# A state-space scan beside experts on one core: exponentials batched by two pairs, rows of B and z moved, norms on GpSimd

## Chip, cores and metric

The kernel runs on one core of one Trainium2 chip. The metric is the device time of one execution in microseconds; the median of three runs is shown for the kernel before. A profile is one execution of its own.

## What is computed

The input x has 2048 tokens of 128 features. Two layers follow each other, each with an attention-like half and a feed-forward half, and ahead of each half a layer norm with a modulation; each half's result is gated and added to x. Cut to what matters here:

```
h = layernorm(x)*(1+ca)+sa ; x = x + ga * retention_and_ffn(h)        # layer 0, first half
h = layernorm(x)*(1+cb)+sb ; x = x + gb * experts(h)                  # layer 0, second half: 8 experts, top 2
h = layernorm(x)*(1+ca')+sa' ; x = x + ga' * mamba(h)                 # layer 1, first half
h = layernorm(x)*(1+cb')+sb' ; x = x + gb' * spectral_product(h)      # layer 1, second half

mamba(h):  xz = h @ W_in.T ; x_val, z = split(xz) ; x_val = silu(conv4(x_val))
           dt = softplus(h[:, :64] @ W_dt.T + b) ; B = h @ W_B.T ; C = h @ W_C.T     # 16 states
           state_n = exp(dt*A_n) * state_n + dt*x_val*B_n      # along the tokens, 256 channels, n = 0..15
           y = sum_n state_n * C_n ; return (y * silu(z)) @ W_out.T
experts(h): p = softmax(h @ w_router) ; out = sum over the top two of p_e * (gelu(h@w1_e + b1_e) @ w2_e + b2_e)
```

## The kernel before, in words

The tokens are cut into four chunks of 512. After layer 0's first half, which is done for all chunks, the rest is one long software pipeline written out by hand in program order on every engine: `later_stages()` (from L255) yields a pair number p, from -12 to 31, and for each p the list of extra stages that run in it. Each engine walks the same list and does its share in order; semaphores tie the engines together.

In pair p two things run side by side.

- **Experts.** Group g = p + 12 is one expert for one chunk (32 groups, so they run in pairs -12 to 19). TensorE makes the hidden layer in four parts k: `up(g, k)` (L1211 on) is three matmuls of 512 columns into one of two banks `pH`. ScalarE's `hidden` (L966) turns each part to gelu, `gel` (L973), a ring of six tiles. `down(g, k)` (L1223 on) multiplies it by the second weights into `pO`: two down products are 16 matmul records of 128 columns in the trace (the line is L1231). VectorE's `moe_acc(g - 1)` (L727, its line L732) adds the previous group's result into X; `down(g, 0)` waits for `moe_acc(g - 1)`. A third `up` waits for the first gelu of its group, since there are two banks.
- **Scan.** Chunk c = p // 8, k = p % 8 covers the states 2k and 2k+1, so pairs 0 to 31 hold four chunks of eight pairs. ScalarE's `decays(p)` (L976) makes the four tiles exp(dt*A), dA (L985; two states by two halves of the channels). TensorE's `row_b(m)` (L1291, matmul L1299) copies row m of B to all partitions of one bank `pB`; VectorE's `products(m)` (L743, L748) multiplies it with u = dt*x into `pCT`; `scans(m)` (L751, L761) does two scans into Hs. GpSimd's `output(p, o)` (L363, L382) multiplies by a row of C (Crow, brought by SyncE's DMAs) to Z. In pairs below ALONE = 20 GpSimd then issues an accumulating DMA, `add_up` (L387, L396), that adds Z to Acc; from pair 20 on TensorE's `total` (L1301 on) adds Z up in PSUM.

The order on VectorE in a pair is product, two scans, `moe_acc(g-1)`, product, two scans, with extra stages between. On TensorE it is given by `pair` (from L1235): two up products, `row_b(2p+1)`, two up products, then `row_b(2p+2)` if the pair has a TensorE stage at place A ("early"), the stages at A, two down products, `row_b(2p+2)` if it wasn't early, the stages at B, two down products, the stages at C. On ScalarE it is four gelus, `decays(p+1)`, then stages at A and B, the norm's application, stages at C. Exp, gelu, silu and softplus are in different tables, so each change between them comes with an ACT_TABLE_LOAD.

The extra stages, for chunk c's tail (chunk c-1 after its scan) and front (chunk c+1 before its scan), by k: tail: `gate` (1), `project` (2, A), `tail_x`, `ln_stats` (2), norm applied and turned (3), `fft` (4, B). Front: norm statistics (4), applied and turned (4, C), the convolution `x_part` (5 A and 6 A), `rows` for B and C (5 B), `dt_part` (6 B, C), `step` (7, makes u), `z_part` (7 A, B). A layer norm goes: VectorE statistics (L538, L541), GpSimd 1/sqrt in four small instructions (`ln`, L347 to L354), ScalarE applies it (`ln_apply`, L830, line L835), TensorE turns it (L1029), ScalarE evacuates it into h4T. For `rows`, ScalarE copies B and C to BCf (L950) and casts them to ST (L952), and GpSimd splits them by four instructions (L479 to L482) before `row_b` can use them.

After pair 31 a serial tail follows for the last chunk: total, gate (L772), projection (L1334), norm, spectral products (L1342), store.

## Time and profile before

| | |
|---|---|
| median of 3 runs | 605.51 us (605.38 to 606.65) |
| profiled execution | 606.43 us |
| its span, first to last instruction | 604.4 us |
| mean granted TensorE clock | 0.948 |
| busy: PE, DVE, ACT, POOL | 482.4, 428.9, 363.4, 313.2 us |
| scan stretch, first product to last scan | 263.5 to 583.0 us of the span |

PE is TensorE, DVE VectorE, ACT ScalarE, POOL GpSimd, SP SyncE. Busy time is the time in which an engine runs an instruction; matmuls are pipelined and their ends are modelled, so of a run of matmuls the starts say more. The granted clock is TensorE's share of full speed: 1.00 is 2.4 GHz, 0.50 is 1.2 GHz. "idle before, releaser" is how long the engine stood before an instruction, and what ended that. The busy shares are averages over stretches with different limits, so the rows below are taken from single stretches.

### The profile page before, as it was taken

The numbers are of one execution on the slowest core, as the hardware profiler recorded it, in microseconds if no ns is written. First come the engines' busy times: TensorE is split into PE (matmuls) and PEld (weight loads), VectorE is DVE, ScalarE is ACT, GpSimd is POOL, SyncE is SP. The second block draws the span as 40 slices with busy tenths as digits, with TensorE's granted clock in tenths as the row PEclk, the third lists the DMA queues.
The fourth block names the chain that finished last, engine by engine and source line by source line (L and its number), as shares of the span: only waits on it lengthen the run. The fifth ranks groups of instructions, "written<-read, shape, count | busy, mean of one in ns | idle before, by whom it ended". The sixth has DMA issues, their size and how long they took to land.

```text
span 604.4 us, 6869 instructions
## 1 busy us (share of the span) xinstructions
PE 482.4 (80%) x2346; PEld 337.7 (56%) x2346; DVE 428.9 (71%) x723; ACT 363.4 (60%) x507; POOL 313.2 (52%) x220
## 2 busy tenths in 40 slices
PE   3869876769899999979869988789897497667573
PEld 3457544434588886757756677657586443233222
DVE  4766798964534334058997779997879985997961
ACT  0531442224664676689999999799988656634201
POOL 3224976866111011314686649767557946566541
PEclk9986999989999999999999989999989779897797
DMA  8700000000000000401866553765725703111000
GB/s 294 272 1 0 1 1 1 2 0 0 1 0 2 2 1 0 142 1 35 193 147 139 151 139 87 180 136 144 168 75 148 165 20 104 70 63 42 17 0 17
DMA packets 15010, 44.74 MB, mean 74 GB/s; under 512 B 2241, under 2 KB 7745, under 8 KB 12545
## 3 DMA queue, kind: packets, MB, share of 16 engines
q0 software_dynamic: 2448, 17.83, 14.5%
q1 hardware_dynamic: 11952, 25.57, 12.4%
q10 hardware_dynamic: 576, 0.92, 0.5%
q8 instruction: 18, 0.29, 0.2%
q14 instruction: 16, 0.12, 0.1%
HBM read 25.31 MB, written 1.18 MB: 44 GB/s over the span
## 4 chain that ended last, share of the span: by engine, by line
PE 24%; ACT 13%; DVE 12%; issue 6%; POOL 3%; DMA 3%; POOLq 0%; ACTq 0%; DVEq 0%
DVE Hs L761 6%; PE pO L1231 5%; DVE pCT L748 4%; ACT dA L985 3%; PE pY L1274 3%; PE pY L1317 3%; ACT gel L973 3%; PE pH L1219 2%; ACT L985 2%; ACT L973 2%; PE pH L1221 2%; PE pH L1220 2%; ACT ln_x L835 2%; PE pH L1274 2%; DMA Acc<-ZS 1%
## 5 line engine op out<-in xcount | busy, mean ns | idle before, releaser
L1231 PEld LDWEIGHTS pO<-w_e,gel 128*128 128x128 f32 x1024 | 124.8, 195 | 14.2 <-issue 8.8
L1231 PE MATMUL pO<-w_e,gel 128*128 128x128 f32 x1024 | 127.2, 279 | 1.4 <-DVE X L732 1.1
L761 DVE TENSOR_TENSOR_SCAN Hs<-dA,HL,pCT 128x512 f32<-128x512 f32 x96 | 117.7, 1268 | 8.1 <-POOL Zev L382 3.8
L382 POOL TENSOR_TENSOR ZS<-Hs,Crow 128x1024 f32<-128x1024 f32 x32 | 76.5, 2392 | 58.3 <-DVE Hs L761 58.3
L973 ACT ACTIVATE gel<-pH,b_e 128x512 f32<-128x512 f32 x128 | 85.9, 687 | 33.3 <-PE pH L1221 32.6
L985 ACT ACTIVATE dA<-dt,a_neg 128x512 f32<-128x512 f32 x128 | 81.9, 710 | 21.0 <-DVE Hs L761 20.7
L748 DVE TENSOR_TENSOR pCT<-u,pB 128x1024 f32<-128x1024 f32 x64 | 78.3, 1224 | 16.7 <-PE pB L1299 15.5
L1219 PE MATMUL pH<-h2h,w_e1h 128*128 128x512 f32 x128 | 57.8, 452 | 22.6 <-ACT gel L973 21.4
L382 POOL TENSOR_TENSOR Zev<-Hs,Crow 128x1024 f32<-128x1024 f32 x26 | 62.8, 2420 | 16.0 <-DVE Hs L761 15.2
L732 DVE SCALAR_TENSOR_TENSOR X<-pO,wts,X 128x128 f32<-128x128 f32 x128 | 35.9, 343 | 43.2 <-PE pO L1231 43.1
L438 POOL TENSOR_TENSOR ZA<-Qsb,S 128x1024 f32<-128x1024 f32 x16 | 38.0, 2374 | 33.6 <-DVE S L656 32.0
L1221 PE MATMUL pH<-h2h,w_e1l 128*128 128x512 f32 x128 | 51.0, 398 | 0.0
L1220 PE MATMUL pH<-h2l,w_e1h 128*128 128x512 f32 x128 | 50.7, 396 | 0.0
L1299 PE MATMUL pB<-ST,sel 96*128 96x512 bf16 x64 | 25.7, 401 | 30.4 <-DVE pCT L748 27.3
L1219 PEld LDWEIGHTS pH<-h2h,w_e1h 128*128 128x128 f32 x128 | 24.1, 188 | 38.6 <-ACT gel L973 34.4
L835 ACT ACTIVATE ln_x<-X,ln_nb,ln_rs 128x128 f32<-128x128 f32 x48 | 19.7, 480 | 36.8 <-POOL ln_nb L354 36.8
L761 DVE TENSOR_TENSOR_SCAN Hs<-dA,pCT 128x512 f32<-128x512 f32 x32 | 37.3, 1207 | 3.8 <-ACT dA L985 2.1
L899 ACT COPY Qsb<-pCT 128x1024 f32<-128x1024 f32 x16 | 16.2, 1013 | 37.2 <-PE pCT L1107 37.2
L1106 PE MATMUL pH<-qk_hi,pick 128*128 128x512 f32 x32 | 16.7, 523 | 23.5 <-DVE S L656 23.5
L973 ACT ACT_TABLE_LOAD x26 | 33.4, 1283 | 0.5
L1299 PEld LDWEIGHTS pB<-ST,sel 96*128 96x128 bf16 x64 | 6.3, 99 | 47.6 <-DVE pCT L748 37.0
L656 DVE TENSOR_TENSOR_SCAN S<-cols,S,pH 128x512 f32<-128x512 f32 x24 | 30.7, 1280 | 0.8
(225 smaller groups left out, 878.1 us busy)
## 6 DMA issues: line engine op xcount, KB each, us to landing
Crow<-c_rows SPq DMA_DIRECT2D x32, 512.0 KB, 4.0
Acc<-ZS POOLq DMA_DIRECT2D x10, 1024.0 KB, 8.5
Acc<-Zev POOLq DMA_DIRECT2D x7, 1024.0 KB, 7.7
w_e<-in_w_e SPq DMA_DIRECT2D x2, 2048.0 KB, 10.4
X<-in_x SPq DMA_DIRECT2D x4, 256.0 KB, 7.0
out<-h2T SPq DMA_DIRECT2D x4, 256.0 KB, 2.2
S<-in_w_mod ACTq DMA_DIRECT2D x2, 384.0 KB, 4.7
w_cx<-in_conv_row SPq DMA_DIRECT2D x1, 512.0 KB, 9.7
```

The source lines that it names most:

```text
L382: pool.tensor_tensor(Z, Hs[:, 2 * o:2 * o + 2, 0:w], Crow[:, 2 * (p % NCB) + o:2 * (p % NCB) + o + 1, 0:w].to_broadcast([P, ND, w]), ALU.m ...
L438: pool.tensor_tensor(ZA[:, :, :], Qsb[:, 2 * (R % 2):2 * (R % 2) + 2, :], S[:, 2 * r:2 * r + 2, :], ALU.mult).then_inc(s["att_zo"], 1)
L732: ins = vec.scalar_tensor_tensor(Xj, pO[:, j * P:(j + 1) * P], wts[:, c, j * E + e:j * E + e + 1], Xj, ALU.mult, ALU.add)
L748: vec.tensor_tensor(pU[:, :, 0:w], half_of(u, c), pB[:, None, 0:w].to_broadcast([P, ND, w]), ALU.mult).then_inc(s["mam_ub"], 1)
L761: vec.tensor_tensor_scan(Hs[:, 2 * o + d, 0:w], dA[:, 4 * (p % 2) + 2 * o + d, 0:w], pU[:, d, 0:w], HL[:, d, n:n + 1] if c else 0.0, ALU.m ...
L973: nc.scalar.activation(gel[:, n % NG, 0:w], pH[n % 2][:, 0:w], ACT.Gelu_apprx_tanh, bias=b_e1[:, NK * e + k:NK * e + k + 1]).then_inc(s["m ...
L985: nc.scalar.activation(dA[:, 4 * (p % 2) + r, 0:WIDTHS[c]], half_of(dt, c)[:, r % 2, :], ACT.Exp, scale=a_neg[:, r % 2, n:n + 1]).then_inc ...
L1219: mm(pH[n % 2][:, 0:w], w_e1h[:, g % E, part], h2h[:, c, 0:w], start=True, stop=False)
L1220: mm(pH[n % 2][:, 0:w], w_e1h[:, g % E, part], h2l[:, c, 0:w], start=False, stop=False)
L1221: mm(pH[n % 2][:, 0:w], w_e1l[:, g % E, part], h2h[:, c, 0:w], start=False, stop=True).then_inc(s["moe_h"], 1)
L1231: ins = mm(pO[:, j * P:(j + 1) * P], gel[:, n % NG, j * P:(j + 1) * P], w_e2[:, NK * (g % E) + k, :], start=(k == 0 and j == 0), stop=(k = ...
L1299: mm(pB[:, 0:w], sel[:, n:n + 1].to_broadcast([96, P]), ST[:, c % 2, 0:w], start=True, stop=True).then_inc(s["mam_bB"], 1)
```

## The change

- `decays`: in odd pairs p ScalarE does the exponentials of pairs p+1 and p+2, in even pairs none. dA has three slots in place of two, taken by p % 3, and decays(p) waits for the scans of pair p-3, not p-2.
- TensorE's `row_b(2p+2)` comes ahead of all down products also in every even pair.
- `z_part` leaves pair 7 of the chunk before and comes in pair 1 of its own chunk (A and B).
- GpSimd applies the norms (four subtract-and-multiply instructions of 128 columns); two of its small instructions go. It also casts BCf to ST.
- The front's norm is turned in pair 5 at a new place "U", behind `row_b(2p+1)` and between the second and third up product; on ScalarE its evacuation stands between the second and third gelu.
- Zev, ZS and Acc (two slabs) become one tile Zt with three slabs: slab 1 for odd pairs; the accumulator of chunk c and the Z of its even pairs use slabs 0 and 2 in turn. So the first output of a chunk waits for the accumulating DMA of the pair two back, and the output of pair k = 2 waits until the previous chunk is gated.

```diff
-        dA = sb("dA", [P, 2 * 2 * ND, TC])
+        dA = sb("dA", [P, 3 * 2 * ND, TC])
         Hs = sb("Hs", [P, 2 * ND, TC])
-        Zev = sb("Zev", [P, 2 * ND, TC])
-        ZS = sb("ZS", [P, 2 * ND, TC])
+        Zt = sb("Zt", [P, 3, 2 * ND, TC])
...
-            return (2 if p < ALONE else 0) + int(at == "B")
+            return (2 if p < ALONE else 0) + int(at in ("B", "U"))
...
+        def acc_of(c):
+
+            return Zt[:, 2 * (c % 2), :, 0:WIDTHS[c]]
+
+        def z_of(p):
+
+            c, k = divmod(p, NP)
+            if k == 0 and not alone(p):
+                return acc_of(c)
+            return Zt[:, 1 if k % 2 else 2 - 2 * (min(c, ALONE // NP) % 2), :, 0:WIDTHS[c]]
...
@@ -263,16 +270,17 @@
                 plan = []
                 if 0 <= tail:
                     plan += [(1, "mid", "gate", tail), (2, "A", "project", tail), (2, "end", "tail_x", tail),
-                             (2, "end", "ln_stats", tail), (3, "apply", "ln_apply", tail), (3, "C", "ln_turn", tail, 2),
+                             (2, "end", "ln_stats", tail), (3, "C", "ln_turn", tail, 2),
                              (3, "end", "bias", tail), (4, "B", "fft", tail)]
                 if 0 <= front < NL:
-                    plan += [(4, "mid", "ln_stats", front), (4, "apply", "ln_apply", front), (4, "C", "ln_turn", front, 1),
+                    plan += [(4, "mid", "ln_stats", front), (5, "U", "ln_turn", front, 1),
                              (5, "A", "x_part", front, 0), (5, "B", "rows", front), (6, "A", "x_part", front, 1),
-                             (6, "B", "dt_part", front, 0), (6, "C", "dt_part", front, 1), (7, "mid", "step", front),
-                             (7, "A", "z_part", front, 0), (7, "B", "z_part", front, 1)]
+                             (6, "B", "dt_part", front, 0), (6, "C", "dt_part", front, 1), (7, "mid", "step", front)]
+                if c >= 0:
+                    plan += [(1, "A", "z_part", c, 0), (1, "B", "z_part", c, 1)]
                 for q in range(1, NL):
                     at = k - (p + AHEAD - 3 * (q - 1))
-                    plan += [(at, "mid", "ln_stats", q), (at, "apply", "ln_apply", q), (at + 1, "A", "ln_turn", q, 0),
+                    plan += [(at, "mid", "ln_stats", q), (at + 1, "A", "ln_turn", q, 0),
                              (at + 1, "B", "route", q), (at + 2, "A", "turn", q), (at + 2, "B", "weigh", q)]
...
             def ln(c):
                 J = blocks(c)
                 pool.wait_ge(s["ln_stats"], L[0] + 1)
-                pool.wait_ge(s["ln_xn"], L[0])
-                pool.tensor_scalar(ln_nm[:, 0:J], ln_mv[:, 0:J, 0], -1.0, None, ALU.mult)
                 link(pool.tensor_scalar(ln_ve[:, 0:J], ln_mv[:, 0:J, 1], EPS, None, ALU.add))
                 link(pool.tensor_tensor(ln_rs[:, 0:J], ln_ve[:, 0:J], mhalf[:, 0:J], ALU.pow))
-                pool.tensor_tensor(ln_nb[:, 0:J], ln_nm[:, 0:J], ln_rs[:, 0:J], ALU.mult).then_inc(s["ln_rstd"], 1)
+                pool.wait_ge(s["ln_tr"], L[0])
+                for j in range(J):
+                    ins = pool.tensor_scalar(ln_x[:, j, :], rows_of(X, c)[:, j, :], ln_mv[:, j, 0:1], ln_rs[:, j:j + 1],
+                                             ALU.subtract, ALU.mult)
+                ins.then_inc(s["ln_xn"], 1)
                 L[0] += 1
...
+                Z = z_of(p)[:, part, :]
                 if p >= ALONE + 2:
-                    Z = [Zev, ZS][p % 2][:, part, 0:w]
                     pool.wait_ge(s["mam_y"], totals(p - 2))
-                elif k == 0 and not alone(p):
-                    Z = Acc[:, c % 2, part, 0:w]
-                    if c >= 2:
-                        pool.wait_ge(s["mam_y2"], 2 * (c - 1))
-                else:
-                    Z = [Zev, ZS][p % 2][:, part, 0:w]
-                    if p >= 2 and o == 0 and sums(p - 2):
-                        pool.wait_ge(mam_s[p % 2], 16 * sums(p - 2))
+                elif p >= 2 and o == 0 and sums(p - 2):
+                    pool.wait_ge(mam_s[p % 2], 16 * sums(p - 2))
+                if k == 2 and c and p < ALONE + 2 and o == 0:
+                    pool.wait_ge(s["mam_y2"], 2 * c)
...
-                pool.wait_ge(s["mam_st0"], c + 1)
-                pool.wait_ge(s["ln_rstd"], L[0])
+                pool.wait_ge(s["mam_bcs"], c + 1)
+                pool.wait_ge(s["ln_xn"], L[0])
                 for name, count in done.items():
                     if count:
                         pool.wait_ge(s[name], count)
+                link(pool.tensor_copy(st, bc))
                 link(pool.tensor_tensor(st[32:64, :], bc[32:64, :], st[32:64, :], ALU.subtract))
                 link(pool.tensor_tensor(P1[64:96, 0:w], bc[64:96, :], st[64:96, :], ALU.subtract))
                 link(pool.tensor_tensor(bc[64:96, :], bc[64:96, :], st[64:96, :], ALU.subtract))
...
-                if p >= 2:
-                    act.wait_ge(s["mam_sc"], 4 * (p - 1))
+                if p >= 3:
+                    act.wait_ge(s["mam_sc"], 4 * (p - 2))
                 for r in range(4):
                     n = 2 * k + r // 2
-                    nc.scalar.activation(dA[:, 4 * (p % 2) + r, 0:WIDTHS[c]], half_of(dt, c)[:, r % 2, :], ACT.Exp,
+                    nc.scalar.activation(dA[:, 4 * (p % 3) + r, 0:WIDTHS[c]], half_of(dt, c)[:, r % 2, :], ACT.Exp,
...
             for p, stages in later_stages():
                 if 0 <= p + AHEAD < NL * E:
-                    hidden(p + AHEAD, range(NK))
-                if 0 <= p + 1 < NL * NP:
-                    decays(p + 1)
+                    hidden(p + AHEAD, (0, 1))
+                run(p, stages, "U")
+                if 0 <= p + AHEAD < NL * E:
+                    hidden(p + AHEAD, (2, 3))
+                for q in (p + 1, p + 2) if p % 2 else ():
+                    if 0 <= q < NL * NP:
+                        decays(q)
                 run(p, stages, "AB")
-                run(p, stages, ("apply",))
                 run(p, stages, "C")
...
@@ -1239,12 +1233,16 @@
                 if moe:
                     up(g, 0)
                     up(g, 1)
+                if any(at == "U" for at, *_ in stages) and not moe:
+                    run(p, stages, "U")
                 if 0 <= p < NL * NP:
                     row_b(2 * p + 1)
                 if moe:
+                    run(p, stages, "U")
+                if moe:
                     up(g, 2)
                     up(g, 3)
-                early = not moe or any(at == "A" and stage in mine for at, stage, *_ in stages)
+                early = not moe or p % 2 == 0 or any(at == "A" and stage in mine for at, stage, *_ in stages)
                 if moe and early and 0 <= 2 * p + 2 < NL * NS:
                     row_b(2 * p + 2)
```

The other lines rename Zev, ZS and Acc to `z_of(p)` and `acc_of(c)`, take out `ln_apply`, the cast on ScalarE, ln_nm, ln_nb and two semaphores, and put ln_xn in the place of ln_rstd in waits. The dA slot p % 3 stands in the scans (L761) too.

## Rows read from the trace of the kernel before

**Rows 1.** Scan stretch: us, busy us of PE, PEld, DVE, ACT, POOL; clock, DMA.

```profile
263.50:583.00 319.50, 256.35 (x1252) 176.26 (x1251) 277.24 (x383) 238.60 (x324) 201.68 (x125) 0.94 0.42 105
```

**Rows 2.** Timeline of VectorE: start us, us, instruction; first products and waits of single pairs.

```profile
275.92 1.23 DVE L748 TENSOR_TENSOR pCT<-u,pB 128x1024 f32<-128x1024 f32 x1 [1.69 <-PE pB L1299]
...
284.63 1.22 DVE L748 TENSOR_TENSOR pCT<-u,pB 128x1024 f32<-128x1024 f32 x1
...
293.17 1.22 DVE L748 TENSOR_TENSOR pCT<-u,pB 128x1024 f32<-128x1024 f32 x1
...
357.73 1.23 DVE L748 TENSOR_TENSOR pCT<-u,pB 128x1024 f32<-128x1024 f32 x1 [3.19 <-PE pB L1299]
...
504.99 2.45 DVE L761 TENSOR_TENSOR_SCAN Hs<-dA,HL,pCT 128x512 f32<-128x512 f32 x2 [3.45 <-POOL Zev L382]
```

**Rows 3.** Timeline of ScalarE in pair 2, to the load before pair 3.

```profile
288.10 1.27 ACT L973 ACTIVATE gel<-pH,b_e 128x512 f32<-128x512 f32 x2
289.84 1.37 ACT L973 ACTIVATE gel<-pH,b_e 128x512 f32<-128x512 f32 x2 [0.47 <-PE pH L1221]
291.23 1.28 ACT L985 ACT_TABLE_LOAD   x1
...
295.11 1.28 ACT L973 ACT_TABLE_LOAD   x1
```

**Rows 4.** Timeline of TensorE in the same pair: third up product, next group's first.

```profile
288.84 0.50 PE L1219 MATMUL pH<-h2h,w_e1h 128*128 128x512 f32 x1 [1.22 <-ACT gel L973]
...
294.03 0.48 PE L1219 MATMUL pH<-h2h,w_e1h 128*128 128x512 f32 x1
```

**Rows 5.** Timeline of ScalarE in pairs 5 and 6, and pair 7's first gelu.

```profile
323.15 1.28 ACT L940 ACT_TABLE_LOAD   x1
...
326.27 1.28 ACT L973 ACT_TABLE_LOAD   x1
327.56 1.27 ACT L973 ACTIVATE gel<-pH,b_e 128x512 f32<-128x512 f32 x2
...
340.95 0.69 ACT L973 ACTIVATE gel<-pH,b_e 128x512 f32<-128x512 f32 x1
```

**Rows 6.** Timeline of ScalarE in pair 7: z's silu and what follows.

```profile
347.97 1.28 ACT L964 ACT_TABLE_LOAD   x1
...
350.37 1.28 ACT L973 ACT_TABLE_LOAD   x1
```

**Rows 7.** Chain that ended last, in order of time: two down products; the projection.

```profile
336.27 1.78 PE pO L1231 x16
...
373.17 1.79 PE pY L1334 x16
```

**Rows 8.** Timeline of VectorE: expert accumulates of pairs 1 and 19.

```profile
279.78 1.11 DVE L732 SCALAR_TENSOR_TENSOR X<-pO,wts,X 128x128 f32<-128x128 f32 x4
...
467.08 1.12 DVE L732 SCALAR_TENSOR_TENSOR X<-pO,wts,X 128x128 f32<-128x128 f32 x4
```

**Rows 9.** Four stretches about two pauses of TensorE (columns as in 1).

```profile
310.00:313.00 3.00, 1.19 (x11) 1.00 (x9) 2.93 (x5) 3.00 (x7) 1.80 (x2) 1.00 0.54 109
313.00:316.00 3.00, 2.26 (x11) 1.53 (x11) 2.97 (x7) 2.17 (x3) 2.50 (x3) 1.00 0.22 44
350.50:353.50 3.00, 1.11 (x6) 0.93 (x6) 2.84 (x3) 2.52 (x4) 1.29 (x1) 1.00 1.02 216
354.00:357.00 3.00, 3.00 (x16) 3.00 (x15) 0.50 (x2) 2.87 (x5) 2.36 (x1) 0.50 0.27 55
```

**Rows 10.** Timeline of TensorE in pair 8: its first two down products.

```profile
353.95 3.53 PE L1231 MATMUL pO<-w_e,gel 128*128 128x128 f32 x16
```

**Rows 11.** Groups of GpSimd's instructions by line: busy us, mean ns.

```profile
L354 POOL TENSOR_TENSOR ln_nb<-ln_nm,ln_rs 128x4 f32<-128x4 f32 x12 | 2.4, 202 | 0.9
...
L450 POOL TENSOR_TENSOR w_out<-w_out,gates 128x256 f32<-128x256 f32 x1 | 0.7, 729 | 0.0
```

**Rows 12.** Timeline of the tail: the last norm applied by ScalarE.

```profile
595.11 1.65 ACT L835 ACTIVATE ln_x<-X,ln_nb,ln_rs 128x128 f32<-128x128 f32 x4 [24.62 <-POOL ln_nb L354]
```

More of the change, by code:

```diff
@@ L283, in later_stages @@
             for stage in (("A", "total", NL * NP - 1), ("end", "gate", last), ("A", "project", last), ("end", "tail_x", last),
-                          ("end", "bias", last), ("mid", "ln_stats", last), ("apply", "ln_apply", last),
+                          ("end", "bias", last), ("mid", "ln_stats", last),
                           ("A", "ln_turn", last, 2), ("A", "fft", last)):
@@ L395, in add_up @@
                     pool.wait_ge(mam_s[(p - 1) % 2], 16 * sums(p - 1))
-                pool.dma_start(Acc[:, c % 2, :, 0:w], [Zev, ZS][p % 2][:, :, 0:w], accum_op=ALU.add).then_inc(mam_s[p % 2], 16)
+                pool.dma_start(acc_of(c), z_of(p), accum_op=ALU.add).then_inc(mam_s[p % 2], 16)
             link(pool.memset(mhalf[:, :], -0.5))
@@ L497, in gate @@
                 for d in range(ND):
[L498 removed]
+                    pool.tensor_tensor(y2[:, d, 0:w], acc_of(c)[:, d, :], half_of(gz, c)[:, d, :],
                                        ALU.mult).then_inc(s["mam_y2"], 1)
@@ L534, in ln_stats @@
                 Xc = rows_of(X, c)
-                vec.wait_ge(s["ln_rstd"], L[0])
+                vec.wait_ge(s["ln_xn"], L[0])
                 L[0] += 1
@@ L828, in _ @@
             nc.scalar.activation(silu_c[:, :], cols[:, COL["c0"]:COL["c0"] + 2], ACT.Silu).then_inc(s["silu_c_ready"], 1)
-            def ln_apply(c):
-                act.wait_ge(s["ln_rstd"], A[0] + 1)
-                act.wait_ge(s["ln_tr"], A[0])
-                for j in range(blocks(c)):
-                    ins = nc.scalar.activation(ln_x[:, j, :], rows_of(X, c)[:, j, :], ACT.Identity,
-                                               bias=ln_nb[:, j:j + 1], scale=ln_rs[:, j:j + 1])
-                ins.then_inc(s["ln_xn"], 1)
-                A[0] += 1
             def ln(dest, c, m, b, high=None):
@@ L950, in rows @@
                 nc.scalar.copy(BCf[:, c % 2, 0:w], PS[b][0:96, 0:w]).then_inc(s["mam_bcs"], 1)
-                act.wait_ge(s["mam_bcs"], c + 1)
-                nc.scalar.copy(ST[:, c % 2, 0:w], BCf[:, c % 2, 0:w]).then_inc(s["mam_st0"], 1)
             def dt_part(c, d, b):
@@ L996, in run @@
                         continue
-                    if stage == "ln_apply":
-                        ln_apply(c)
-                    elif stage in ("ln_turn", "route", "turn", "x_part", "rows", "dt_part", "z_part"):
+                    if stage in ("ln_turn", "route", "turn", "x_part", "rows", "dt_part", "z_part"):
                         {"ln_turn": turned, "route": route, "turn": turn, "x_part": x_part, "rows": rows, "dt_part": dt_part,
@@ L1312, in total @@
                 first = k == 0 or p == ALONE
-                Z = [Zev, ZS][p % 2]
+                Z = z_of(p)
                 for o in range(2):
@@ L1316, in total @@
                     for d in range(ND):
-                        ins = mm(pY[d][:, 0:w], ident[:, :], Z[:, 2 * o + d, 0:w], start=(first and o == 0),
+                        ins = mm(pY[d][:, 0:w], ident[:, :], Z[:, 2 * o + d, :], start=(first and o == 0),
                                  stop=(k == NP - 1 and o == 1))
@@ L1323, in total @@
                         for o in range(2):
-                            ins = mm(pY[d][:, 0:w], ident[:, :], Acc[:, c % 2, 2 * o + d, 0:w], start=False, stop=False)
+                            ins = mm(pY[d][:, 0:w], ident[:, :], acc_of(c)[:, 2 * o + d, :], start=False, stop=False)
                 ins.then_inc(s["mam_y"], 1)
```

12 lines of the change are left out of this document (3 added, 9 removed).

## The prediction

> **What bounds the kernel now.** I read the busy table of the joint and lone scan stretches first [rows 1]: from the first product of pair 0 to the last scan of pair 31, 319.5 us pass, VectorE works in 277.2 of them and is the busiest engine by 20 us. So what a change can take out of this stretch is VectorE's idle time, 42.3 us; behind it lies a serial tail of 604.4 - 583.0 = 21.4 us. Next VectorE's own order in time [rows 2]: from pair 2's first product to pair 3's, 293.17 - 284.63 = 8.54 us pass, a plain pair without a pause. The pauses stand at the seams of the chunks: 1.69 us for a row of B ahead of pair 1, 3.19 us for one ahead of pair 9.
>
> That bound has little air under it. ScalarE in pair 2 [rows 3] goes from the first gelu (288.10) to the next pair's (296.40, behind the load at 295.11) in 8.30 us, with no pause but those for TensorE's up products: gelus until 291.23 (3.13), a table load and four exponentials until 295.11 (3.88), a load back until 296.40 (1.29). While ScalarE does the 5.17 us of exponentials and loads, TensorE does the down products, which it has begun some 2.2 us after the first gelu, and from 294.03 on the next group's first up products [rows 4]. So today one engine's work covers the other's in every pair.
>
> **Part 1, exponentials of two pairs in odd pairs.** Removed: one exp and one gelu load per two pairs, 2 x 1.28 = 2.57 us of ScalarE [rows 3]. The same eight exponentials remain. What matters is the chain. In an odd pair ScalarE needs 3.13 for gelus, then 1.29 + 2 x 2.59 + 1.29 = 7.76 for load, eight exponentials and load: 10.89 until the even pair's first gelu. In the even pair no exponential covers TensorE. The down products of a group come behind its last up products, which wait for its gelus; the next group's first up product comes behind the down products; so all is in series: first gelu to first up product of the next group 294.03 - 288.10 = 5.93 (row of B and down products in it), and 1.00 from an up product's start to its gelu (288.84 in [rows 4] to 289.84 in [rows 3]). That is 6.93. The new chain is 10.89 + 6.93 = 17.8 us for two pairs. Today's is 2 x 8.30 = 16.6, VectorE needs 2 x 8.54 = 17.1. Two loads go, and the chain gets longer, because TensorE's 5.9 us that lay beside the exponentials now lie behind them every second time. In plain pairs the bound passes from VectorE to this loop of ScalarE and TensorE.
>
> The loop from pair 1 to pair 19 is nine periods: 9 x 17.8 = 160.2. What stages add inside it: pairs 5 and 6, the conv's silu with load and the copy of B and C, 326.27 - 323.15 less the cast, 2.5; the evacuation of the turned norm between gelus, taken at 0.6; and pair 6, whose convolution and step products stand between its gelus and the next, 340.95 - 327.56 = 13.39 in place of 6.93 [rows 5], so 9.6, twice (pairs 13 and 14): 19.1. Pairs 9 and 10, the moved z's silu with its load, 350.37 - 347.97 = 2.4 [rows 6], and the projection ahead of pair 10's down products, 1.79 [rows 7]: 4.2, twice (17 and 18): 8.4. Pairs 11 and 12: evacuation 0.8, spectral products 0.9 (half as many matmuls as the projection): 1.7. Sum 189.4 us.
>
> Today VectorE's expert accumulate of pair 1 starts at 279.78 and that of pair 19 at 467.08, 187.3 apart [rows 8]. That is the point at which VectorE waits for the loop, so the change makes this stretch 189.4 - 187.3 = 2.1 longer, from a start that is 1.7 earlier (part 2). Net 0.4 later at pair 19.
>
> **The clock.** In that loop TensorE stands still between the even pair's first two up products and its first gelu: 10.89 less 2.2 (up products of the odd pair) plus 0.7, less some 5.7 of work, 3.7 us. In the trace a pause of 2.2 us, TensorE's wait to turn the norm behind pair 4, left the granted clock at 1.00 (2.4 GHz); the wait for pair 8's first gelu, some 2 us too, was followed by half of it (0.50, the 1.2 GHz level) [rows 9]. And the half group of down products behind that wait took 3.53 us [rows 10] in place of 1.78 [rows 7]. The trace prices one such fall at 1.75 at most, and at nothing if it lies inside the wait. A 3.7 us pause is longer than the one that cost this, and what follows it (up, down, up) is all in the loop. It comes in pairs 0, 2, 4, 8, 10, 12, 16 and 18. The 187.3 of today hold two such falls (pairs 8 and 16); the 189.4 hold none. Bounds 0 and 8 x 1.75 = 14; I take 1.0 each, since part of the low stretch can lie in the pause and VectorE has a little air in pairs 4 and 12: 8.0. TensorE: Matmul & The Clock Gate, section HAM oscillation — how this bites in real kernels, of the Trainium skill says that a kernel whose matmul groups are parted by waits pays the fall anew at every group, the extra being half of the throttled time. By that rule alone all eight would be paid in full, nearer the upper bound; the rows show one such pause that goes unpunished, and decide for less.
>
> **Part 2, row of B ahead of the down products in even pairs.** It takes away the waits that follow even pairs, 1.69 ahead of pair 1 [rows 2] and 3.19 ahead of pair 9. The first counts in full (1.7). The second is already inside the loop's sum. In plain pairs the row is in time either way. Cost: none on TensorE, which has the same matmuls in another order; if the product ahead is late the down products wait for it, under 1.3 us and hidden while VectorE waits for the loop.
>
> **Part 3, z in its own chunk's pair 1.** A move of 2.4 us of ScalarE and four matmuls from pair 7 to pair 9. It frees pair 8 and loads pair 9, both in the sum. In chunk 0 it leaves pair -1, where it makes room for the four extra exponentials (2.6 against 2.4). In chunk 3 it lies in a pair that VectorE bounds: nothing.
>
> **Part 4, norms and cast on GpSimd.** Per norm GpSimd loses two small instructions (0.5) and gets four of 128 columns. No row shows one. Bounds 0.20 (4 columns) and 0.73 (256 columns, two inputs) [rows 11]; I take 0.46, between them by columns: 1.8. Inside the loop GpSimd has room. In the tail it replaces 1.65 on ScalarE [rows 12] plus 0.6 of small ones and hand-overs: gain 0.4, bounds -0.8 and +1.2. GPSIMD Engine Reference, section Engine selection, of the Trainium skill says that with one input it is roughly as fast as VectorE, slow only with two; by that the tail would gain near 1 us. The cast costs GpSimd up to 1.15, ScalarE loses 0.62; in pair 21 the two about cancel. The third Z slab and the waits on the accumulating transfers add no wait that the loop does not cover. From pair 20 to the tail I take no change: there are no expert products and ScalarE has room.
>
> **Sum:** 0.4 + 8.0 - 0.4 = +8.0. The profiled execution took 606.43 (span 604.4), so 614.4; the median of the runs shown is 0.9 lower, 605.51, so **613.5 us**.
>
> **Rivals.** A: the clock holds, since TensorE's work shifts until no pause is long enough. For: the first two stretches of [rows 9], where a pause costs nothing. Against: its last two, and that the new pauses are longer. Then 0.4 - 0.4 and up to 2 us of slack that I rounded into the loop: 603 to 606, 604.
> B: the loop is not closed, because VectorE's order keeps TensorE fed and the saved loads and early rows are all that counts. Then the pauses at the seams go: 1.7, and at pairs 6 to 8 and 14 to 16 the 3.19 ahead of the next pair and some 1.4 for a late accumulate, 4.6 each: -11, 594.5. Against: the series of gelu, down product, up product in an even pair has no other way round.
> C: GpSimd's late rows of B and C. The copy that feeds them now stands behind eight exponentials (2.6 later), then five instructions, and two outputs behind them; VectorE's scan already waited 3.45 us for this in pair 23 [rows 2]. It decides once the outputs of pair 6 end later than that pair's down products, some 3 us from now; then +2 a chunk on top, 619.
> D: gains at the seams and losses in plain pairs cancel within 0.2%.
>
> **How the numbers follow.** Forecast 0.50, C 0.13: slower 0.63. A 0.19 and B 0.12 with a few hundredths for a shorter loop: faster 0.30 (A ends on the other side). D: 0.07. What this kernel's runs can tell from no change is about 0.2%, 1.2 us. Range: clock bounds put 605.5 to 619.4 around the sum; the low end takes in A and the near part of B, the high end most of C: 599 to 619. Slower holds most of the chance; its own range is 607 to 619.
>
> **What would show it.** The odd pair's first gelu to the next odd pair's: 17.8 to 19.5 us in plain pairs. ScalarE's waits for up products and VectorE's expert accumulate waiting for down products in odd pairs grow, waits for rows of B fall; stretches of half clock appear in pairs 2 and 4, where now there are none; table loads fall by some 20. Wrong, if the accumulate of pair 19 comes earlier than 465, or if VectorE runs the plain pairs at 8.54 still.

## The result and the profile after

Four runs of the changed kernel have a median of **631.25 us** (629.32 to 633.41), four of the kernel before beside them 606.08 us. The ratio is 1.0419 (95% interval 1.0387 to 1.0452): slower by 4.2%, where 613.5 us was forecast and the range ended at 619. The direction was right, the size about a third of what came, and 631 lies outside the range.

The profiled execution took 629.32 us with a span of 627.3, so 22.9 us more span than before. The page's busy rows, time slices and chain, of the kernel after:

```profile
span 627.3 us, 6814 instructions
...
PE 498.2 (79%) x2346; PEld 348.6 (56%) x2346; DVE 429.9 (69%) x723; ACT 314.9 (50%) x435; POOL 347.6 (55%) x248
...
PEclk9979998899899999987989997889988879887796
...
PE 46%; DVE 22%; ACT 17%; issue 6%; POOL 6%; DMA 1%; ACTq 0%; POOLq 0%; DVEq 0%
```

ScalarE works 48.5 us less (363.4 before) and VectorE 1.0 us more, so nothing got more work but GpSimd. The same 2346 matmuls keep TensorE busy 15.8 us longer (482.4 before). The chain that ended last, as the profile follows it back, has TensorE in 77 of the 185.5 us of the loop before and in 107 of the 207.1 us of the loop after (the loop is bounded below). Both point at TensorE as the place where the time went; the timelines show how.

The stretch of [rows 1], from the first product of pair 0 to the last scan (columns as there), and then the loop from pair 1's first gelu to pair 19's:

```profile
263.66:604.30 340.64, 269.92 (x1235) 184.49 (x1235) 278.48 (x383) 198.58 (x275) 219.32 (x140) 0.88 0.40 99
...
278.44:485.51 207.07, 173.33 (x937) 134.16 (x936) 162.30 (x249) 142.71 (x195) 135.15 (x90) 0.90 0.54 128
```

VectorE has the same work as in [rows 1] (278.48 and 277.24 us) in 340.64 in place of 319.50 us: its idle time went from 42 to 62 us. The loop took 207.07 us; between the same gelus of the kernel before (279.79 to 465.32) it is 185.53 us at a mean clock of 0.98, here 0.90. The accumulates that answer to [rows 8], in VectorE's timeline after:

```profile
277.75 1.13 DVE L739 SCALAR_TENSOR_TENSOR X<-pO,wts,X 128x128 f32<-128x128 f32 x4 [0.28 <-PE pO L1225]
...
486.96 1.12 DVE L739 SCALAR_TENSOR_TENSOR X<-pO,wts,X 128x128 f32<-128x128 f32 x4
```

So pair 1 comes 2.0 us earlier, pair 19 comes 19.9 later, and the end 22.9 later. The loss is in the joint pairs. Here is how one period of it looks, in ScalarE's timeline from pair 2 to pair 4 (it answers to [rows 3]):

```profile
291.61 1.26 ACT L966 ACTIVATE gel<-pH,b_e 128x512 f32<-128x512 f32 x2
294.03 0.69 ACT L966 ACTIVATE gel<-pH,b_e 128x512 f32<-128x512 f32 x1 [1.16 <-PE pH L1215]
295.31 0.69 ACT L966 ACTIVATE gel<-pH,b_e 128x512 f32<-128x512 f32 x1 [0.59 <-PE pH L1215]
301.39 1.37 ACT L966 ACTIVATE gel<-pH,b_e 128x512 f32<-128x512 f32 x2 [5.39 <-PE pH L1215]
303.12 1.38 ACT L966 ACTIVATE gel<-pH,b_e 128x512 f32<-128x512 f32 x2 [0.36 <-PE pH L1215]
304.52 1.28 ACT L978 ACT_TABLE_LOAD   x1
305.82 5.02 ACT L978 ACTIVATE dA<-dt,a_neg 128x512 f32<-128x512 f32 x8
310.85 1.28 ACT L966 ACT_TABLE_LOAD   x1
312.14 1.26 ACT L966 ACTIVATE gel<-pH,b_e 128x512 f32<-128x512 f32 x2
```

The reader sees both halves of the forecast's loop. From pair 3's first gelu to pair 4's 10.75 us pass with one short wait of 0.36 (forecast 10.89). From pair 2's to pair 3's 9.78 us pass (forecast 6.93, plus 1.0 for the clock), and ScalarE stands still for 5.39 of them, waiting for the next group's first up product. TensorE's timeline at the start of that even pair:

```profile
292.35 0.79 PE L1213 MATMUL pH<-h2h,w_e1h 128*128 128x512 f32 x1 [4.32 <-ACT gel L966]
292.94 0.63 PE L1214 MATMUL pH<-h2l,w_e1h 128*128 128x512 f32 x1
...
295.52 5.13 PE L1225 MATMUL pO<-w_e,gel 128*128 128x128 f32 x32
300.41 0.48 PE L1213 MATMUL pH<-h2h,w_e1h 128*128 128x512 f32 x1
```

TensorE waits 4.32 us for the gelu behind eight exponentials (forecast 3.7; in pairs 4 and 8 it is 3.70), and comes out of the pause at half clock. The ranges of the two legs (columns as in [rows 1]):

```profile
291.60:301.40 9.80, 9.05 (x43) 7.90 (x44) 5.07 (x9) 2.65 (x5) 5.11 (x3) 0.65 0.79 179
301.40:312.10 10.70, 7.78 (x50) 6.23 (x48) 9.94 (x22) 10.29 (x14) 6.04 (x4) 1.00 0.35 82
```

The even pair runs at a granted clock of 0.65, the odd one at 1.00. [Rows 9] had 1.00 as well as 0.50 behind two pauses of about 2 us; the second experiment below shows a loss in each of the eight pairs with a longer one (3.4 to 4.3 us).

### The profile page after: what moved, and what is told of

The parts are those of the page before. It is cut to its first block, busy times and chain, and to the rows that moved or that the text cites. A ratio compares the mean times of both kernels' runs of the same rounds, so it can differ in the third digit from the quotient of the medians.

```text
span 627.3 us, 6814 instructions
## 1 busy us (share of the span) xinstructions
PE 498.2 (79%) x2346; PEld 348.6 (56%) x2346; DVE 429.9 (69%) x723; ACT 314.9 (50%) x435; POOL 347.6 (55%) x248
## 4 chain that ended last, share of the span: by engine, by line
PE 46%; DVE 22%; ACT 17%; issue 6%; POOL 6%; DMA 1%; ACTq 0%; POOLq 0%; DVEq 0%
PE pO L1225 12%; ACT dA L978 6%; PE pY L1315 5%; PE pH L1213 4%; DVE S L663 4%; PE pH L1215 3%; DVE Hs L768 3%; PE pH L1214 3%; PE pY L1272 3%; ACT gel L966 3%; DVE pCT L755 3%; DVE pH L662 2%; POOL Zt L388 2%; ACT L966 2%; ACT L978 2%
## 5 line engine op out<-in xcount | busy, mean ns | idle before, releaser
L388 POOL TENSOR_TENSOR Zt<-Hs,Crow 128x1024 f32<-128x1024 f32 x64 | 153.0, 2392 | 106.7 <-DVE Hs L768 102.9
L1225 PEld LDWEIGHTS pO<-w_e,gel 128*128 128x128 f32 x1024 | 126.9, 199 | 12.7 <-issue 8.7
L755 DVE TENSOR_TENSOR pCT<-u,pB 128x1024 f32<-128x1024 f32 x64 | 78.4, 1224 | 23.1 <-PE pB L1297 22.4
L1213 PE MATMUL pH<-h2h,w_e1h 128*128 128x512 f32 x128 | 61.9, 484 | 37.8 <-ACT gel L966 36.8
L1215 PE MATMUL pH<-h2h,w_e1l 128*128 128x512 f32 x128 | 54.9, 429 | 0.0
L1214 PE MATMUL pH<-h2l,w_e1h 128*128 128x512 f32 x128 | 54.7, 427 | 0.0
L1315 PE MATMUL pY<-Zt,ident 128*128 128x512 f32 x96 | 52.3, 694 | 2.9 <-POOL Zt L388 2.9
L1297 PE MATMUL pB<-ST,sel 96*128 96x512 bf16 x64 | 27.9, 435 | 31.1 <-DVE pCT L755 27.4
L362 POOL TENSOR_SCALAR ln_x<-X,ln_mv,ln_rs 128x128 f32<-128x128 f32 x48 | 37.6, 793 | 1.3
L1315 PEld LDWEIGHTS pY<-Zt,ident 128*128 128x128 f32 x96 | 21.6, 227 | 27.9 <-issue 22.3
L1100 PE MATMUL pH<-qk_hi,pick 128*128 128x512 f32 x32 | 16.6, 519 | 22.0 <-DVE S L663 22.0
L845 ACT ACTIVATE h3T<-pH,mods 128x512 f32<-128x512 f32 x3 | 2.3, 777 | 59.6 <-PE pH L1023 59.6
## 6 DMA issues: line engine op xcount, KB each, us to landing
w_e<-in_w_e SPq DMA_DIRECT2D x2, 2048.0 KB, 10.5
```

Source lines behind the costliest of these rows:

```text
L362: ins = pool.tensor_scalar(ln_x[:, j, :], rows_of(X, c)[:, j, :], ln_mv[:, j, 0:1], ln_rs[:, j:j + 1], ALU.subtract, ALU.mult)
L388: pool.tensor_tensor(Z, Hs[:, 2 * o:2 * o + 2, 0:w], Crow[:, 2 * (p % NCB) + o:2 * (p % NCB) + o + 1, 0:w].to_broadcast([P, ND, w]), ALU.m ...
L755: vec.tensor_tensor(pU[:, :, 0:w], half_of(u, c), pB[:, None, 0:w].to_broadcast([P, ND, w]), ALU.mult).then_inc(s["mam_ub"], 1)
L1213: mm(pH[n % 2][:, 0:w], w_e1h[:, g % E, part], h2h[:, c, 0:w], start=True, stop=False)
L1214: mm(pH[n % 2][:, 0:w], w_e1h[:, g % E, part], h2l[:, c, 0:w], start=False, stop=False)
L1215: mm(pH[n % 2][:, 0:w], w_e1l[:, g % E, part], h2h[:, c, 0:w], start=False, stop=True).then_inc(s["moe_h"], 1)
```

## The experiments

**The batch of exponentials, undone and judged by itself.** One edit to the changed kernel, on ScalarE; all other parts stay:

```
-                for q in (p + 1, p + 2) if p % 2 else ():
+                for q in (p + 1,):
```

> The changed kernel with the exponentials of one pair in every pair again (the third dA slab, the early row of B, the moved z and GpSimd's norms and cast stay). Theory 1 (the closed ScalarE-TensorE loop of Part 1 with its clock falls is the whole loss): each odd pair to the next odd pair goes back from 20.3-20.7 us to about 17.1, first gelu of pair 1 to that of pair 19 from 207 to about 185, time 603 to 608 us. Theory 2 (GpSimd's norms and late rows, or z in pair 1, cost most): it stays above 620 us.

Measured: 603.2 us, ratio to the kernel before 0.9941 (0.9915 to 0.9968). One line is worth 28 us, and what is left of the change beats the kernel before. From pair 1's first gelu to pair 19's it is 181.94 us (277.89 to 459.83), at a mean granted clock of 1.00; theory 1 holds, and the stretch is 3 us shorter than its 185. Its plain pair 8, in ScalarE's timeline:

```profile
348.37 1.27 ACT L966 ACTIVATE gel<-pH,b_e 128x512 f32<-128x512 f32 x2
...
351.50 1.28 ACT L978 ACT_TABLE_LOAD   x1
352.80 2.56 ACT L978 ACTIVATE dA<-dt,a_neg 128x512 f32<-128x512 f32 x4
355.38 1.28 ACT L966 ACT_TABLE_LOAD   x1
356.67 1.27 ACT L966 ACTIVATE gel<-pH,b_e 128x512 f32<-128x512 f32 x2
```

A pair takes 8.30 us again, loads included. The two loads that the batch saves per two pairs (2.57 us) bought a period of 10.75 + 9.78 us in place of 16.6.

**The pauses filled.** Is the loss the longer loop or the clock? In even pairs, except those that hold the convolution, TensorE repeats its second up product five times before the real one (0.70 us each in the trace, 3.5 in all). The repeats write the same values to the same bank, which nobody reads before the last, so they only keep TensorE at work in the pause:

```
+                for _ in range(again):
+                    mm(pH[n % 2][:, 0:w], w_e1h[:, g % E, part], h2h[:, c, 0:w], start=True, stop=False)
+                    mm(pH[n % 2][:, 0:w], w_e1h[:, g % E, part], h2l[:, c, 0:w], start=False, stop=False)
+                    mm(pH[n % 2][:, 0:w], w_e1l[:, g % E, part], h2h[:, c, 0:w], start=False, stop=True)
...
-                    up(g, 1)
+                    up(g, 1, 5 if p % 2 == 0 and p % NP != 6 and p >= 0 else 0)
```

> The changed kernel, with TensorE repeating the second up product five times (5 x 0.64 = 3.2 us) in the pause of pairs 0, 2, 4, 8, 10, 12, 16, 18, ...; nothing else moves. Theory 1a (beyond the 17.8 us loop the loss is the clock, 1.6 to 3 us a fall): the half-clock stretches of these pairs go, plain periods fall from 20.3-20.7 to about 18.0 us, time 612 to 618 us. Theory 1b (the clock is a side effect, the loop is longer in itself): period stays at 20 us or more, time 629 us or more.

Measured: 616.48 us, ratio 1.0153 (1.0098 to 1.0209). More work on TensorE made the kernel 15 us faster. Its loop, and TensorE's timeline in pair 8:

```profile
277.58:472.42 194.84, 183.28 (x1042) 142.08 (x1041) 162.95 (x253) 143.37 (x194) 135.24 (x89) 0.99 0.57 132
```

```profile
355.10 0.50 PE L1217 MATMUL pH<-h2h,w_e1h 128*128 128x512 f32 x1 [0.21 <-ACT gel L966]
...
356.84 3.73 PE L1229 MATMUL pO<-w_e,gel 128*128 128x128 f32 x32
360.33 0.48 PE L1217 MATMUL pH<-h2h,w_e1h 128*128 128x512 f32 x1
```

The loop takes 194.84 us at a clock of 0.99 in place of 207.07 at 0.90. From the third up product to the next group's first one it is 360.33 - 355.10 = 5.23 us; in pair 2 of the changed kernel, above, 300.41 - 292.35 = 8.06. The legs (from a pair's first gelu to the next pair's) that start in an even pair, us:

| pair | 0 | 2 | 4 | 8 | 10 | 12 | 16 | 18 | sum |
|---|---|---|---|---|---|---|---|---|---|
| changed kernel | 8.54 | 9.78 | 9.75 | 8.28 | 11.23 | 9.30 | 9.55 | 10.28 | 76.7 |
| filled | 6.91 | 7.61 | 7.50 | 6.94 | 9.26 | 8.33 | 6.94 | 9.26 | 62.8 |

The difference is 14.0 us in eight legs, 1.75 each. The plain even legs of 6.91 and 6.94, with the odd legs of 10.76 to 10.78, are the forecast's full-clock loop: 17.7 where 17.8 was forecast.

The repeats don't reach a ninth fall. In pair 13 TensorE waits for VectorE ahead of a row of B, in the changed kernel and in the filled one, and the convolution's products behind it run at half clock. The batched kernel with the norms on ScalarE and the row late (its run stands further down) has the same wait and stays at 1.00. TensorE's timelines of the changed kernel, the filled one, and that one:

```profile
417.58 0.39 PE L1297 MATMUL pB<-ST,sel 96*128 96x512 bf16 x1 [1.83 <-DVE pCT L755]
417.81 5.30 PE L1272 MATMUL pY<-h3T,w_cx 128*128 128x512 f32 x8
```

```profile
408.09 0.39 PE L1301 MATMUL pB<-ST,sel 96*128 96x512 bf16 x1 [1.83 <-DVE pCT L755]
408.31 5.29 PE L1276 MATMUL pY<-h3T,w_cx 128*128 128x512 f32 x8
```

```profile
416.67 0.39 PE L1312 MATMUL pB<-ST,sel 96*128 96x512 bf16 x1 [1.84 <-DVE pCT L755]
416.90 3.60 PE L1287 MATMUL pY<-h3T,w_cx 128*128 128x512 f32 x8
```

The leg of pair 13 is 15.25 us in the first two and 13.56 in the third: 1.7 us for this fall.

**Only half of them filled.** The same with `p in (0, 2, 4, 8)` as the condition.

> The changed kernel with the five repeats of the second up product only in pairs 0, 2, 4 and 8; the pauses of pairs 10, 12, 16 and 18 stay empty. Theory 1 (each fall has its own price, paid in its own pair): pairs 0, 2, 4, 8 take 6.9 to 7.6 us from first gelu to the next pair's, pairs 10, 12, 16, 18 stay at 9.3 to 11.2; about half of the filled kernel's gain, 622 to 626 us. Theory 2 (the repeats help in another way, by moving the whole loop against GpSimd and VectorE once): over 80% or under 20% of that gain.

Measured: 620.74 us, ratio 1.0237 (1.0188 to 1.0285). The filled pairs take 6.94, 7.58, 7.49 and 6.93 us, the empty ones 11.62, 9.42, 9.67 and 10.30: each fall is paid in its own pair, by 7.4 us in these four legs against 14.0 in all eight. The total of 620.74 us lies below theory 1's range, and its gain, 10.5 of 14.8 us or 71%, fits neither theory; in the profiled executions 1.8 us of it arose ahead of pair 0, which is no effect of the edit (its first gelu starts at 268.13, in the changed kernel at 269.90). So the legs answer the question, for theory 1, and the total alone would not.

**The norms back on ScalarE**, each at its old place, the cast still on GpSimd. The central lines of the edit:

```
-                for j in range(J):
-                    ins = pool.tensor_scalar(ln_x[:, j, :], rows_of(X, c)[:, j, :], ln_mv[:, j, 0:1], ln_rs[:, j:j + 1],
-                                             ALU.subtract, ALU.mult)
+                for j in range(blocks(c)):
+                    ins = nc.scalar.activation(ln_x[:, j, :], rows_of(X, c)[:, j, :], ACT.Identity,
+                                               bias=ln_nb[:, j:j + 1], scale=ln_rs[:, j:j + 1])
```

> The changed kernel with the norms on ScalarE again (each at its old place; the cast stays on GpSimd). Theory 1 (only the tail and the one or two places where VectorE waited for GpSimd see it): 1 to 2 us faster, 629.5 to 630.5. Theory 2 (GpSimd's 3.2 us a norm delay its outputs and the rows in the loop): 5 us or more faster, 626 or less.

Measured: 628.44 us, ratio 1.0356 (1.0294 to 1.0418), 2.8 us less by the medians with intervals that overlap, and 0.5 us less span; that lies between the two theories and decides for neither. The part that can be read without doubt is the tail. GpSimd's timeline there, of the changed kernel, and the group of its norm instructions:

```profile
614.45 0.23 POOL L358 TENSOR_SCALAR ln_ve<-ln_mv 128x4 f32<-128x4 f32 x1
614.77 1.04 POOL L359 TENSOR_TENSOR ln_rs<-ln_ve,mhalf 128x4 f32<-128x4 f32 x1
615.91 3.13 POOL L362 TENSOR_SCALAR ln_x<-X,ln_mv,ln_rs 128x128 f32<-128x128 f32 x4
```

```profile
L362 POOL TENSOR_SCALAR ln_x<-X,ln_mv,ln_rs 128x128 f32<-128x128 f32 x48 | 37.6, 793 | 1.3
```

Four of them take 3.13 us where ScalarE took 1.65 [rows 12]. From the last update of X to the last addition it is 623.38 - 612.35 = 11.03 us; in the run with the norms on ScalarE 10.15, in the kernel before 10.14. The move costs the tail 0.9 us, where a gain of 0.4 was forecast. The rule of the Trainium skill that the forecast named (GPSIMD Engine Reference, Engine selection: with one input about as fast as VectorE) does not hold for this form: 128 columns took 793 ns, more than 256 columns with two inputs [rows 11], while VectorE needs 339 ns for the same operation on 128 columns (L605 of the changed kernel, 16 of them). For the cast it does by the nearest row: 603 ns for 512 columns, where VectorE's product takes 1224 ns for 1024.

**The row of B late again in even pairs** (`p % 2 == 0 or` taken out).

> The changed kernel with the row of B behind the down products again in even pairs. Theory 1 (the row only counted ahead of pair 1 and at the seams): 1.7 us slower ahead of pair 1, at most 3 in all, 632 to 634 us. Theory 2 (in a loop with air the early row only delays down products of even pairs by about 0.4 us each): 0 to 4 us faster, 627 to 631.

Measured: 626.02 us, ratio 1.0317 (1.0264 to 1.037): 5 us faster than the changed kernel, past the end of theory 2. Ahead of the loop theory 1 was right all the same: pair 0's first product starts at 263.67 in both, pair 1's accumulate at 279.64 in place of 277.75, so the early row was worth 1.9 us there. From that accumulate to pair 19's it is then 203.72 us in place of 209.21 (by the gelus 203.48 for 207.07). Two legs gain most: pair 10 takes 8.73 us for 11.23, pair 13 13.56 for 15.25, both at a clock of 1.00 where the changed kernel had a fall, although TensorE still pauses for 2.81 us ahead of pair 10's third up product; pair 12 takes 1.2 us more. Over the whole kernel the early row was a loss here, and the part that the legs show came by the clock.

**The same three parts, where exponentials come in every pair.** Three kernels, each the first experiment's with one more part undone, and the kernel before with the early row alone.

> The first experiment's kernel (exponentials of one pair in every pair) with the norms on ScalarE as well. Theory 1 (the norms cost the 0.89 us that the tail shows, and GpSimd has room elsewhere): about 1 us faster than that kernel, 601 to 603 us. Theory 2 (the four exponentials and the norm crowd ScalarE in pair 4, GpSimd is the better place inside the loop): equal or up to 2 us slower, 603 to 605.

Measured: 600.8 us, ratio 0.9904 (0.9871 to 0.9938). Against 603.2 this goes theory 1's way, just past its 601, though the two intervals overlap a little.

> The first experiment's kernel with z in pair 7 of the chunk before, as before the change. Theory 1 (the move only shifts 2.4 us of ScalarE from one pair to another): within 1.5 us of that kernel, 602 to 605 us. Theory 2 (freeing pair 8 of the moved z is what makes that kernel faster than the kernel before): 605 us or more. Theory 3 (the 2.4 us in pair 1, where ScalarE has no air, are a loss): 601 us or less.

Measured: 607.82 us, ratio 1.0017 (0.999 to 1.0044). Theory 2: with z back in pair 7 all of the gain is gone. VectorE's timeline at the start of pair 9 shows one of the places:

```profile
354.34 1.22 DVE L754 TENSOR_TENSOR pCT<-u,pB 128x1024 f32<-128x1024 f32 x1
357.43 2.45 DVE L767 TENSOR_TENSOR_SCAN Hs<-dA,HL,pCT 128x512 f32<-128x512 f32 x2 [1.87 <-issue]
```

ScalarE's timeline of that kernel has the exponentials of pair 9 at 356.01, late by the z that ran at 349.18 and its load. The row of B is there in time, the exponentials aren't. From pair 8's first product to pair 9's it is 9.71 us in place of 8.96, from pair 16's to pair 17's 9.62 in place of 8.95, and from pair 0's to pair 1's, where z of chunk 0 now stands ahead, 10.64 in place of 8.66. These three make 3.4 us; the rest of the loss was not taken apart.

> The first experiment's kernel with the row of B behind the down products in even pairs, as before the change. Theory 1 (the early row removes VectorE's waits of 1.69 us ahead of pair 1 and 3.19 us ahead of pair 9): 2 to 6 us slower, 605 to 609 us. Theory 2 (the waits go over to the expert accumulates, which then wait for the down products): within 1 us, 602 to 604.

Measured: 600.92 us, ratio 0.9904 (0.9873 to 0.9934): not slower, if anything 2 us faster, which is also outside theory 2's range. Theory 1 fell.

> The kernel before with one edit: the row of B ahead of all down products in even pairs. Theory 1: the seam waits go, 2 to 5 us faster than the kernel before (601 to 604 us). Theory 2 (they pass to the accumulates): within 1 us of it, about 606.

Measured: 605.95 us, ratio 0.9989 (0.9965 to 1.0014): nothing, theory 2. Two waits of its VectorE, ahead of pair 1 and pair 9, tell why:

```profile
278.00 2.33 DVE L761 TENSOR_TENSOR_SCAN Hs<-dA,pCT 128x512 f32<-128x512 f32 x2 [1.96 <-ACT dA L985]
...
357.22 1.23 DVE L748 TENSOR_TENSOR pCT<-u,pB 128x1024 f32<-128x1024 f32 x1 [0.95 <-PE pB L1299]
```

The wait of 1.69 us for the row of B [rows 2] is gone, and all of it stands one instruction later as a wait for exponentials (1.96, before 0.19): pair 2's first product comes 285.30 - 264.17 = 21.13 us after pair 0's, before 284.63 - 263.51 = 21.12. The 3.19 ahead of pair 9 fell to 0.95, but pair 9 comes only 1.2 us earlier, since pair 4 took 12.44 us from its first gelu to the next pair's, before 11.43. There the early row opened a pause of its own, and half clock followed it (0.50 from 310.3 to 313.6). TensorE's timeline:

```profile
309.70 0.39 PE L1299 MATMUL pB<-ST,sel 96*128 96x512 bf16 x1 [1.89 <-DVE pCT L748]
```

In the kernel before the same pair has a pause of 2.2 us, and the clock stays at 1.00 [rows 9].

**z in its own chunk, alone and in the batched kernel.** First the kernel before with the two z entries of the plan moved from pair 7 to pair 1, then the changed kernel with them moved back.

> The kernel before with z moved to its own chunk's pair 1, nothing else. Theory 1 (the move is a gain by itself: it frees pair 8, where VectorE waits 3.19 us for the row of B behind a late gelu): 3 to 5 us faster, 601 to 603 us. Theory 2 (it only pays with the dA third slab and the early rows): within 1.2 us of 606.

Measured: 604.39 us, ratio 0.9969 (0.9943 to 0.9996): a gain of 1 to 2 us (1.2 by the medians, 1.9 by the ratio), between the theories.

> The changed kernel with z in pair 7 of the chunk before again. Theory 1 (in the closed loop z only changes its pair): pair 1 to 2, 9 to 10 and 17 to 18 take 10.8 in place of 13.2 us, pair 7 to 8 and 15 to 16 take 13.2 in place of 10.8, and so does pair -1 to 0; time within 3 us of 631. Theory 2 (the move is a gain here too, as with exponentials in every pair): 634 us or more.

Measured: 626.98 us, ratio 1.0354 (1.032 to 1.0389), 4 us faster than the changed kernel and 1 us below theory 1's range; theory 2 fell. The legs are theory 1's: pairs 1 to 2, 9 to 10, 17 to 18 take 10.78, 10.76, 10.76 us, pairs -1, 7 and 15 take 13.14, 13.16, 13.17. In the closed loop the same move that gained 4.6 us with exponentials in every pair loses 4: there it lets pair 9's exponentials come in time, among other places; here z stands in three legs between pairs 1 and 19 in place of two, and no leg has room. That is 2.4 us of the loop's 4.6 (202.52 against 207.07 us); the other 2.2 lie in the even legs (74.5 us in all eight in place of 76.7, most of it in pairs 10 and 16), with 34 us of the loop at half clock in place of 41. Why the falls came out shorter was not taken apart.

**What is best.** Three kernels have the norms on ScalarE and the row late; the first two with exponentials in every pair, the third with the batch:

> The changed kernel without three of its parts: exponentials in every pair, norms on ScalarE, the row of B late. What is left of the change is the moved z, the cast on GpSimd and the third dA slab. If the three undone parts are independent: 0.994 less 0.004 less 0.004 of the kernel before, 597.5 to 600 us, faster than both kernels. If the norm and the row delay the same chain: 600 to 602.

Measured: 600.44 us, ratio 0.9923 (0.9898 to 0.9949). The undone parts don't add up: the higher of the two ranges came.

> The kernel of the run before it with the cast of B and C back on ScalarE. Theory 1 (0.6 us of ScalarE twice against 1.15 us of GpSimd, about even): within 1.5 us of it. Theory 2 (rival C of the prediction, GpSimd's rows of B and C are late): 2 us or more faster.

Measured: 600.56 us, ratio 0.9922 (0.9895 to 0.9949). The cast is even, theory 1. For rival C this says little, since the copy that feeds GpSimd stands behind four exponentials here and not behind eight.

> The changed kernel with the exponentials of two pairs kept, norms on ScalarE and the row of B late. Theory 1 (the batch is the loss, the rest only trims): 621 to 625 us, over 20 us slower than the kernel with exponentials in every pair. Theory 2 (the loop was made long by the norm and the row): 615 us or less.

Measured: 623.46 us, ratio 1.0286 (1.0255 to 1.0316), 23 us behind the same kernel with exponentials in every pair. Theory 1.

So the kernels with z in its own chunk, three dA slabs, the norm turned between the gelus of pair 5, and exponentials in every pair lie at 600.4 to 603.2 us, 0.6 to 1.0% faster than the kernel before; between the best four the runs don't decide. Neither the norms on GpSimd nor the early row of B gained anything in them, so both can stay as they were.

## Why the prediction was wrong in its size

Against its own execution the span grew by 22.9 us; the forecast was 8.0. By its steps, with the accumulates of pairs 1 and 19 as marks (in the filled kernel they start at 278.70 and 474.19, 195.5 us apart):

| step | forecast | measured | from |
|---|---|---|---|
| pair 1 earlier | -1.7 | -2.0 | 277.75 against 279.78 |
| loop with the eight pauses filled | +2.1 | +8.2 | 195.5 less 187.3 |
| clock falls behind those pauses | +8.0 | +13.7 | 209.2 less 195.5 |
| pair 19 to the end | -0.4 | +3.0 | 22.9 less 19.9 |

The direction came from the loop, and that mechanism was right. Two terms of the sum were too small by about the same amount, the clock by 5.7 us and the loop by 6.1; the end adds 3.4. (Between the gelus of pairs 1 and 19 the eight falls make 12.2 us of difference and not 13.7; pair 0's lies ahead of those marks.)

- **The loop** was found, and where it closes: 17.7 us in plain pairs (17.8 forecast). Its total was 6 us short. The largest miss is an oversight: z of chunk 0 moves into pair 1 as well, and the leg from pair 1 to 2 takes 13.18 where 10.8 was reckoned, 2.4 us. The forecast charged this in pairs 9 and 17 only. The period from pair 13 to 15 takes 28.74 in the filled kernel, 1.4 more than forecast, and the fall in pair 13, which was not in the forecast's list, is 1.7: that part of the row belongs to the clock. Of the rest, up to 0.7 us in single even legs, some is the early row, which Part 2 had as hidden: in the filled kernel's pair 2 it waits for VectorE's product and holds the down products up by 0.5 us. Some is the repeats' own, 0.3 us in pair 10, where the third up product stands behind them.
- **The clock** is the failed step that weighs most: with the ninth fall 15.4 us where 8.0 was forecast. The eight pairs were named rightly (0, 2, 4, 8, 10, 12, 16, 18, all of them fell), and the pause of 3.7 us too. The price of 1.0 each was not: 1.75 is measured on the mean (1.0 to 2.6), which is the bound that the forecast held as its upper end. The bound's size was right by luck: it was taken from half a group of down products, while a fall here stretches the up products too: in pair 2 from 292.35 to 295.52, 3.17 us, against 1.74 in pair 8 of the filled kernel (355.10 to 356.84), and the down products from 3.49 to 4.89; others, as pair 8 with 1.3 us, cost less than the bound. The reason given for 1.0, that part of the low stretch lies in the pause and VectorE has air, wasn't shown by any row, and TensorE was busy in 36 of the loop's 41 us at half clock. With all eight paid at 1.75 the sum would have been 619.5, still some 12 under the measured median: this step alone doesn't explain the miss. The forecast set the full price aside because one pause of 2.2 us went unpunished [rows 9]; but the runs have pauses of 1.8 to 2.8 us on both sides, so that row could not decide, and the eight longer ones that the batch opened were all paid. The rule of the Trainium skill (TensorE: Matmul & The Clock Gate, HAM oscillation), that each group behind a wait pays anew, was the nearer.
- **The row of B** (Part 2) gained nothing by itself, since the wait of 1.69 us covered one for exponentials. In the changed kernel pair 1's exponentials come with pair 0's, and there the early row gave 1.9 us ahead of pair 1, as the run with the row late shows. So the forecast's 1.7 came true, for a reason that it had not seen: the row needed the batch. What it had at no cost, the row inside the loop, cost more than that.
- **The tail** came out 1.5 us longer by the last product's distance to the end (26.7 against 25.2 us), 0.9 of it the norm on GpSimd, taken at 0.46 us an instruction and measured at 0.79. Another 1.5 us lie between pair 20's first product and the last one (108.6 against 107.1), where no change was forecast; no run settles them, and 0.6 us between the last addition and the end stays open too.
- **Of the rivals**, A fell (clock 0.90 in the loop), and with it D. B fell; its seam gains are real only where the loop is not closed, and then they come from the moved z. C's wait is there, its price is not: VectorE waits 0.30 us for the row ahead of pair 8's first product, and a scan of pair 7 waits 2.92 us for GpSimd's output behind the rows (at 342.27; the longest such wait in the loop before is 0.46), but pairs 6 and 7 take 13.40 and 10.77 us as before (13.39 and 10.72). No run has the cast on ScalarE beside the batch.
- **Of what was to be seen**, a half clock in pairs 2 and 4, more waits of ScalarE for up products (58.3 us from pair 1 to pair 19, before 13.8) and fewer loads came true. Of the three plain periods one, 19.05 us (pair 7 to 9), lies in the 17.8 to 19.5 of the forecast; the others took 20.50 (3 to 5) and 20.31 (15 to 17). That VectorE would wait less for rows of B did not: 11.7 us against 7.5 from pair 1's first gelu to pair 19's, since a row of an even pair now stands behind TensorE's pause (the one for pair 3, issued at 295.08 in pair 2, cost VectorE 3.50 us).

## What to carry to other kernels

Batching work of one kind on an engine saves its switches, but the work that used to lie beside it on the other engine then lies behind it in the pair that has none: draw both engines' chain over the whole period before you count loads. Where two engines hand work to and fro, every pause that such a batch opens on TensorE is to be priced with the clock over all that follows it until the next hand-over, up and down products both. A row or copy moved forward in TensorE's order can open such a pause too, where what frees its bank comes late. And before a wait is booked as a gain, look at which other input of the same or the next instruction comes second.

## What the runs showed of the hardware

More matmuls made the kernel faster: 11% more of them in the loop (1042 recorded against 937) raised the granted clock from 0.90 to 0.99 and took 12.2 us out of it. In the changed kernel's loop some 0.10 x 207 x 2 = 41 us ran at the 1.2 GHz level, in the filled one 4; 12.2 of the 37 us of difference were paid, a third. The rule of the Trainium skill (TensorE: Matmul & The Clock Gate, HAM oscillation) gives half of the throttled time, by an estimate from it 18 us; the trace is below it. That TensorE waited in part of the low stretches explains little: it was busy in 36 of the 41 us. Some of what the full clock gives back the filled kernel loses at other waits, as in pair 2 above; the rest is open.

Pauses of TensorE of 1.8 to 2.8 us went both ways: 1.89 us ahead of pair 8 in the kernel before and 1.83 in pair 13 of the changed one were followed by half clock, as was one of 2.83 in pair 18 with the row late; 2.19 in pair 4 of the kernel before, 1.84 in pair 13 of the last batched kernel, 2.81 in pair 10 with the row late and 3.33 in pair 12 with exponentials in every pair were not. The eight of 3.42 to 4.32 us in the changed kernel all were. No run here settles what decides it. And GpSimd needed 793 ns for 128 columns with two operands per partition, VectorE 339 ns for the same, and GpSimd 603 ns for a cast of 512.
